# Deferring the 24 weight transposes behind the first statistics, and moving the trA evacuation from ScalarE to VectorE

## What is computed

```python
xn = _layernorm(x)                       # over the 1024 features
# recurrent layer
xr = _rmsnorm(xn, norm_w)
f = max(sigmoid(xr @ w_forget.T), 0.9);  v = xr @ w_input.T;  o = sigmoid(xr @ w_output.T)
h = f * h + (1 - f) * v                  # per head a 128 x 128 state, scan over time
s = xn + o * h.sum(-1)
# mixture of 4 experts, one per token
e = argmax(xn @ W_router)
y = gelu(xn @ W1[e] + b1[e]) @ Wo + bo + xn
g = silu(_layer_norm(y))
return x + s * g
```

## Time and profile before

| | us |
|---|---|
| median of 2 runs | 3403.75 |
| the two runs | 3294.16 and 3513.35 |
| the profiled execution, its own time | 3300.66 |
| its span on core 5, the slowest core | 3298.8 |
| spans of the 8 cores | 3266.0 to 3298.8 |
| mean granted TensorE clock of the cores | 0.959 to 0.961 |

### The profile page before, as it was taken

One profiled execution on the slowest core, in us unless ns is written; L12 is line 12 of the kernel. 1 busy time (PEld: TensorE's weight loads), 2 busy tenths in 40 slices (PEclk: granted clock), 3 DMA queues, 4 the chain that ended last, 5 costly groups with the idle time before them and its releaser, 6 DMA issues.

```text
span 3298.8 us, 32661 instructions; the slowest of 8 cores (3266.0 to 3298.8 us)
## 1 busy us (share of the span) xinstructions
PE 2863.9 (87%) x13376; PEld 1262.5 (38%) x13376; DVE 687.8 (21%) x1225; ACT 506.4 (15%) x797; POOL 212.7 (6%) x285
## 2 busy tenths in 40 slices
PE   0048778787999999999999999999999999999994
PEld 0023344332444444444444444444444344444442
DVE  0036666651002100310111012002200210021003
ACT  0033433320001110020102011101110111102001
POOL 1015442400000000000000000000000000000000
PEclk9998888898999999999999999999999999999997
DMA  9999999904434444444354435444444444343432
GB/s 136 106 127 121 135 141 149 120 28 172 147 140 165 154 153 153 166 141 164 130 181 149 155 140 179 153 144 144 172 166 144 175 136 158 141 166 141 161 146 77
DMA packets 262385, 476.14 MB, mean 144 GB/s; under 512 B 204700, under 2 KB 204700, under 8 KB 216988
## 3 DMA queue, kind: packets, MB, share of 16 engines
q1 hardware_dynamic: 63296, 402.69, 35.4%
q0 software_dynamic: 173600, 65.07, 18.4%
q10 hardware_dynamic: 25344, 6.29, 2.2%
HBM read 482.44 MB, written 81.79 MB: 171 GB/s over the span
## 4 chain that ended last, share of the span: by engine, by line
PE 72%; DVE 2%; DMA 1%; ACT 1%; issue 0%; DVEq 0%; SPq 0%; ACTq 0%; POOL 0%; POOLq 0%
PE pre L607 55%; PE y2a L628 7%; PE y2b L628 7%; PE pre L614 2%; DMA w1sl<-w1s 1%; DVE y L664 0%; DVE y L660 0%; DVEq L96 0%; DVE maskedA L709 0%; PE y2b L633 0%; PE y2a L633 0%; PE pmu L641 0%; ACT g_bf L746 0%; PE psq L564 0%; PE pmu L557 0%
## 5 line engine op out<-in xcount | busy, mean ns | idle before, releaser
L607 PE MATMUL pre<-maskedA,w1sl 128*128 128x512 bf16 x8192 | 1823.3, 381 | 23.2 <-DVEq L96 12.4
L607 PEld LDWEIGHTS pre<-maskedA,w1sl 128*128 128x128 bf16 x8192 | 784.0, 98 | 996.2 <-issue 95.9
L770 ACT ACTIVATE interA<-pre 128x512 bf16<-128x512 f32 x256 | 152.9, 597 | 1726.8 <-PE pre L614 1726.6
L408 PE MATMUL trA<-ident_bf,xn_tm 128*128 128x128 bf16 x256 | 35.2, 282 | 243.0 <-DVEq L96 209.3
L628 PE MATMUL y2a<-interA,wosl 128*128 128x512 bf16 x1024 | 238.6, 394 | 1.1 <-ACTq L96 1.1
L628 PE MATMUL y2b<-interA,wosl 128*128 128x512 bf16 x1024 | 226.2, 379 | 0.0
L162 POOL DMA_DIRECT2D w1s<-w x256 | 189.0, 786 | 274.4 <-issue 274.4
L703 DVE COPY mask_bf<-pmb 4x512 bf16<-4x512 bf16 x8 | 3.3, 412 | 951.3 <-PE pmb L574 951.3
L544 POOL DMA_DIRECT2D out<-y x8 | 6.0, 745 | 2628.3 <-DVEq L96 2628.3
L628 PEld LDWEIGHTS y2a<-interA,wosl 128*128 128x128 bf16 x1024 | 102.6, 101 | 133.5 <-issue 21.4
L628 PEld LDWEIGHTS y2b<-interA,wosl 128*128 128x128 bf16 x1024 | 100.1, 98 | 120.9 <-issue 0.5
(11 more groups left out here) (114 smaller groups left out, 1245.6 us busy)
## 6 DMA issues: line engine op xcount, KB each, us to landing
w1sl<-w1s SPq DMA_DIRECT2D x256, 1024.0 KB, 4.9
wosl<-wos SPq DMA_DIRECT2D x64, 1024.0 KB, 5.7
w1s<-w POOLq DMA_DIRECT2D x256, 128.0 KB, 16.0
x_a<-x SPq DMA_DIRECT2D x8, 2048.0 KB, 14.2
x_b<-x SPq DMA_DIRECT2D x8, 2048.0 KB, 17.9
out<-y POOLq DMA_DIRECT2D x8, 2048.0 KB, 7.7
wos<-wo POOLq DMA_DIRECT2D x8, 1024.0 KB, 45.1
xnbf_s<-xn_fm SPq DMA_DIRECT2D x8, 1024.0 KB, 16.8
```

Source lines behind the costliest of these rows:

```text
L408: ins = te.transpose(trA[p_][:, sub * 128:(sub + 1) * 128], xn_tm[:, sub * D + k * 128: sub * D + (k + 1) * 128], ident_bf[:, :])
L607: ins = te.matmul(pre[b][:, :], w1sl[gi % 2][:, off:off + 128], maskedA[:, (e * KC + k) * TT:(e * KC + k + 1) * TT], start=first, stop=False)
L770: ti(sc.activation(interA[:, i_abs * TT:(i_abs + 1) * TT], pre[b][:, :], AF.Gelu), "pre_F%d" % b, 1)
```

## The change

Two edits, both in block A.

1. The 24 DMA transposes, with their wait for `wnat_s`, become a function that ACT calls after `accums(0)`, `sqrtf(0)` and `accums(1)`, ahead of the loop over stages, in place of first of all.
2. The eight copies of `trA` to `xn_fm` go from ACT to VectorE, as `tensor_copy`, each just ahead of the evacuation of `trB` for the same k. The waits of the copies (`s_xnw`: the store of the same buffer two stages ago; `sv_s`) go with them. One drain at the end of VectorE's evacuation now raises both `ss_xnev` and, by an empty instruction after it, `sv_x2ev`; ACT's drain goes.

```diff
-                    W(sc, "s_wnat", 48)
-                    for widx in range(3):
-                        for k in range(KC):
-                            ti(sc.dma_start_transpose(
...
+                    def wt_transposes():
+                        W(sc, "s_wnat", 48)
+                        for widx in range(3):
+                            for k in range(KC):
+                                ti(sc.dma_start_transpose(
...
                     accums(0)
                     sqrtf(0)
                     accums(1)
+                    wt_transposes()
                     for t in range(NT):
                         if t + 1 < NT:
                             sqrtf(t + 1)
-                        W(sc, "s_xnw%d" % (t % 2), 16 * (t // 2))
-                        W(sc, "sv_s", t - 1)
-                        for k in range(KC):
-                            g_ = 8 * t + k
-                            p_ = g_ % 2
-                            W(sc, "trA_R%d" % p_, g_ // 2 + 1)
-                            ti(sc.copy(xn_fm[t % 2][:, k * TT:(k + 1) * TT], trA[p_][:, :]),
-                               "trA_F%d" % p_, 1)
-                        DR(sc, "ss_xnev")
...
                     for t in range(NT):
+                        W(v, "s_xnw%d" % (t % 2), 16 * (t // 2))
+                        W(v, "sv_s", t - 1)
                         for k in range(KC):
                             g_ = 8 * t + k
                             p_ = g_ % 2
+                            W(v, "trA_R%d" % p_, g_ // 2 + 1)
+                            ti(v.tensor_copy(xn_fm[t % 2][:, k * TT:(k + 1) * TT],
+                                             trA[p_][:, :]), "trA_F%d" % p_, 1)
                             W(v, "trB_R%d" % p_, g_ // 2 + 1)
                             ti(v.tensor_scalar(xn2_fm[:, k * TT:(k + 1) * TT], trB[p_][:, :],
                                                norw_cm[:, k:k + 1], None, OP.mult),
                                "trB_F%d" % p_, 1)
-                        DR(v, "sv_x2ev")
+                        DR(v, "ss_xnev", "sv_x2ev")
```

More of the change, by code:

```diff
@@ L196, in _ @@
                 def _(sc):
-                    W(sc, "s_wnat", 48)
-                    for widx in range(3):
-                        for k in range(KC):
-                            ti(sc.dma_start_transpose(
-                                wTs[widx][:, k * D:(k + 1) * D],
-                                wnat_s[widx * D:(widx + 1) * D, k * 128:(k + 1) * 128]),
-                               "s_wt", 16)
+                    def wt_transposes():
[3 more added lines that the diff above has]
+                                ti(sc.dma_start_transpose(
+                                    wTs[widx][:, k * D:(k + 1) * D],
+                                    wnat_s[widx * D:(widx + 1) * D, k * 128:(k + 1) * 128]),
+                                   "s_wt", 16)
                     def accum_piece(t, i):
```

## The result

The changed kernel takes 3324.02 us (median of 12 runs), the kernel before 3300.87 us (median of 10), a ratio of 1.0086 with a 95% interval of 1.0065 to 1.0107: some 28 us slower (21 to 35), clear of the noise and below the 2% that I had named as distinguishable. In some runs the cores of one die are slower than the others whatever the kernel; the ratios leave such runs out, means for cores 0 to 3 or 4 to 7 alone leave such a die out, and the medians hold them. With ten runs the kernel before stands where its profiled execution stood, and not at the 3403.75 us of the first two. The profiled execution of the changed kernel took 3322.33 us (span 3320.4 on core 3, the slowest; the cores lie between 3292.4 and 3320.4): 21.7 us more than the one of before.

What follows compares the result with a forecast made beforehand. Compute, not POOL's casts, was taken to end block A, so microseconds lost there count in full. Start +15, cold TensorE +2 and evacuation +6 made +23 us on 3300.66: 3324 us, +0.7%, own range 3312 to 3340, wide range 3300 to 3440.

Steps and rivals of the forecast that it cites:

- The term for the evacuation: Block A's stages: eight more copies on VectorE lengthen each evacuation by 0.9 us, +6 us over seven stages (0 to +13).
- rival (d): Evacuation becomes a VectorE-TensorE ping-pong, +7.8 us each, with slow-clock projections: +88 us in all, 3389 us; chance 0.07.
- 0.86 for the same: Whole kernel: chance given to a difference under about 2% (66 us of 3300); faster 0.04, slower 0.10.
- Start, +15.0: Start of block A: transposes begin 44.7 us later, stream ends at 236.6, first projection starts there instead of 221.6.
- The two corrections whose sum I had set at zero: Start: bias loads without transposes as neighbours, up to -9.6 us, against the third x load sharing engines with the stream.
- Rival (a): The start costs nothing: biases 9.6 us earlier, stream helped by a dry q0; +10 us, 3311 us; chance 0.21.
- Cold TensorE, +2: First projection: after some 100 us idle its 64 matmuls run slower, 16.29 against 13.97 us; taken as +2 us.
- the smaller term: Evacuation on VectorE: +6 us at a spacing of 0.39 us, rather than +13 at 0.48 by the drain rule.
- Rival (b): Transpose stream at the start squeezed to its slow pace throughout, a third queue running: +43 us, 3344 us; chance 0.13.
- Rival (c): Transposes at the start run as if alone, 51 us for the stream: -49 us, 3252 us; chance 0.04.
- Rival (e): ACT's copies in the evacuation weren't on the path, so freeing ACT gives nothing; already in the sum, no separate chance.
- The range's upper end, 3440: Whole kernel's time: high end of the range, past 3344 and 3389, allowing for two timings 219 us apart.

## Why the prediction was right in size, and where it was wrong

The time was 3324.0 forecast and 3324.02 measured; against the forecast of +0.7%, some 23 us, the ratio says +0.86%, some 28. That the times agree to the last digit is luck, as the steps show.

- **The step that failed.** The term for the evacuation, +0.9 us a stage, priced VectorE's pace and the late group and put the clock of the projection behind them at nothing: a slow clock was to come only with rival (d), whose evacuation takes 0.85 us an instruction. The runs show it at 0.33 to 0.43 us an instruction. The evacuation itself cost 0.69 us, less than the term, and 0.45 us more went into the router and the first projection, since 17 of 56 first projections begin slow in place of 2. Over seven stages that is 4.8 and 3.1 us, less 0.7 in the rest of the stage, against 6 forecast.
- **What was called undecidable.** The prediction took a difference under 2% for one that can't be told from none, and its chances were built on that: 0.86 for the same. The interval of 0.65% to 1.07% tells it from none. The two timings that lie 219 us apart were no measure of the noise of a comparison, whose interval is 0.2% to either side. That the kernel before really stands near its profiled 3300.66 us and not at 3403.75 was read rightly.
- **Start, +15.0.** Right, +15.0 on the mean and +13.9 on the slowest core, and made as written: the transposes wait for bo_cm and the statistics, the first projection for their landing, with TensorE idle for 115 us. The transposes began at 106.8 (104 to 115 forecast). The last landing was to be near 237 and was at 235.4 on core 3 (225.2 + 10.2). The two corrections whose sum I had set at zero are both there and small: the biases came 3.3 us earlier, and the stream took 3.1 us longer, 116.9 against 113.8 on the mean (core 5's 122.8 was the forecast's value). How long a stream takes is itself uncertain: the deferral alone had the same start, 106.9, and a stream of 109.0, which made its first projection only 7.2 us late on the mean. In the number 15.0 there is luck. Rival (a), in which the start costs nothing, counted on 9.6 us from the biases, and got 3.3.
- **Cold TensorE, +2.** Right: +1.6.
- **Evacuation, +0.9 a stage, +6.** The stage grew by 1.04 us, +7.3 in all, and this step was right for half its reasons. The evacuation itself takes 0.69 us: 0.29 for the group that ACT used to free early (0.36 by the run that puts it back), as the prediction said, and the rest for VectorE's tail (0.19) and for the semaphore that now comes behind the last L308 (0.20), which the prediction had not separated ("somewhat more than the larger"). The other 0.45 us is the first projection's clock, in 17 of 56 stages, for about 1.5 us each. Rival (d)'s ping-pong didn't come, its clock did.
- **The Trainium skill on VectorE.** By the rule of the Trainium skill, "VectorE: DVE Perf Modes", section "The DRAIN you can't avoid", that the next instruction waits for the empty pipe, the evacuation should have cost 1.9 us a stage, an estimate of the prediction. The same section adds that an instruction that isn't held starts earlier, which the prediction left out. L305 follows L308 after 0.39 us and L308 follows L305 after 0.34, with 0.48 and 0.42 us of length, both inputs ready: the trace differs from the rule and agrees with what is added to it, and the smaller term was the right one.
- **Rival (b), the stream squeezed to 143 us** by a third queue: no. The load of x ran beside it in the changed kernel too, and the stream took 116.9.
- **Rival (c), the transposes as if alone.** Not in this change; but its mechanism is the largest thing in block A. Holding the casts back gives 3252.32 us, and I had priced (c) at 3252. The digits agree by luck: the first projection starts 67.4 us earlier than before (141.6 on the mean), 10 more than (c) had, and block B only 51.6 us earlier, since the casts then land at 679.1, behind the end of computing at 677.1. That competition was there before and after, so the change couldn't touch it.
- **Rival (e).** Right as far as it goes: ACT's copies weren't on the path. The kernel with only the copies moved shows no gain from a freer ACT, and costs 0.34%.
- **What was to stay.** The last w1s lands at 649.9 on the mean, far ahead of the block's end, and block B kept its length within 0.5 us, both as forecast.
- **The range's upper end, 3440,** came from two timings 219 us apart. The median of twelve runs didn't need that width.

The recorded expectations missed mostly in one direction: they took more from a single move than it gave. The deferral alone was to pay for ACT's late copies, and the wait for the landing hid them; the late bias wait and SP as issuer were to give the whole shift of the transposes, and the stream, which shares its engines with the casts, gave part of it back; casts in block B were to gain 22 us and gained nothing. Two missed the other way: the moved copies alone cost 3314.54 us where 3308 was expected, and the waiting casts gave 3252.32 where it was 3275.

What stays open: what sets the moment at which the clock comes back, and so in how many stages of a kernel and on which die it falls again; and what sets the stream's length between 109 and 123 us at equal load.

## What to carry to other kernels

Before a long stream of transfers is put behind other work, look for what that work waits for: here 27 us of computing were to be hidden, and a wait for four small bias loads, which neither side needed yet, came along and made 20 of the 38 us by which the stream was put off. Ask next whom the stream shares the DMA engines with: the same 24 transposes took 117 us beside casts that nobody needed yet, and 41 to 50 us once these waited. And work moved onto an engine that stands between TensorE and its next work costs more than its own time, since TensorE's groups become sparser and the clock of the following matmuls can fall.

## What the runs showed of the chip that was not expected

- DMA transposes beside the casts hold the engine that issues them: 1.3 us an issue when q0 is empty, 3 to 6 us and more beside it. An engine with computing to do loses that time; SP had nothing else to do then.
- Matmuls with unread output, placed in waits, can keep up the clock of what follows: 13.60 us instead of 15.27 for the third projection, 5.03 instead of 5.65 for the evacuation with copies on ACT. In front of groups paced by VectorE they did not: 40 of 56 first projections began slow, against 17 without them.
- Casts in block B cost it 15 to 22 us (2544 to 2551 against 2529), most of it in its first tile, which takes 322 to 325 us in place of 307 to 310 on cores 4 to 7. The DMA engines have room in block B as a whole (a share of 0.43 to 0.44 from 900 us on), but not there: from 670 to 740 us, while the casts ran on core 5, their share was full and TensorE was busy for 49.8 of 70 us.
